# Causal attention core: looks at plain heads moved behind the hyperbolic ones, row maxima turned and laid in two goes

## The chip, the cores and the metric

The program runs on one core of one Trainium2 chip. Its time is device microseconds (us) of that core. The kernel before took 5732.23 us, the median of three runs (5721.1, 5732.23, 5742.0). The engines are named as the profile names them: PE (TensorE matmul), PEld (its weight load), DVE (VectorE), ACT (ScalarE), POOL (GpSimd), SP (SyncE). Each engine works off its own instructions in the order in which they are written, and waits on semaphores for the others.

## The reference

A batch of 32 sequences of 273 tokens by 256 channels passes a patch embedding, a plain causal attention, a quantised feed-forward, then the attention that this change is about, then a second attention (not causal) with a mixture of experts. The attention that matters has 16 heads of three kinds, all causal:

```python
def _hyp_attn(q, k, v, curv):                          # heads 6 to 9
    tq = jnp.sqrt(1.0 / curv + jnp.sum(q * q, axis=-1, keepdims=True))
    tk = jnp.sqrt(1.0 / curv + jnp.sum(k * k, axis=-1, keepdims=True))
    inner = jnp.einsum('bhtd,bhsd->bhts', q, k) - tq * jnp.swapaxes(tk, -1, -2)
    arg = jnp.maximum(-curv * inner, 1.0 + 1e-07)
    dis = jnp.sqrt(1.0 / curv) * jnp.arccosh(arg)
    scores = 1.0 / (eps + dis) + _causal_bias(...)
    return jnp.einsum('bhts,bhsd->bhtd', softmax(scores), v)
outs.append(_sdpa(q[:, :6], k[:, :6], v[:, :6], 1.0 / math.sqrt(HD)))   # heads 0 to 5, plain
outs.append(_hyp_attn(q[:, 6:10], k[:, 6:10], v[:, 6:10], curvature))
outs.append(_sdpa(qn, kn, v[:, 10:], math.sqrt(HD)))                     # heads 10 to 15, q and k of unit length
```

A softmax needs its row maximum subtracted. Heads 10 to 15 need none, since their scores are bounded. For the other ten the kernel finds the maxima of a batch ahead of its main pass.

## The kernel before, in words

`attention_core` runs twice: as "g" (causal, the three kinds, tiles g_...) and as "e" (not causal, all plain, tiles e_...). Both go through 32 batches of three query tiles of 91 tokens. `program` cuts each batch into 16 slots (p = 0 to 15). In slot p every engine's `step` is called three times: "post" for the batch before, "main" for the current one, "pre" for the next. A piece of work has a step number: -16 to -1 is "pre" of that slot plus 16, 0 to 15 is "main", 16 to 31 is "post". An engine's order is thus slot by slot, and in a slot post, main, pre; inside one call it is the order in which `step` is written.

The work of a batch n in "g":

- **Look** at head h (lines 1526 to 1535 for PE, 1656 to 1697 for DVE). PE makes the scores by query into a ring of three PSUM banks, in two units. For a plain head DVE reduces them to the negated row maximum (`g_neg`, L1670, three instructions). For a hyperbolic head DVE reduces (L1668), copies the raw scores by key (L1683), clamps (L1689) and forms the argument of a root (L1694). Then ACT takes the root one slot later (ROOT, L1614 and L1616), DVE adds (SUM, L1700, two slots later) and ACT makes the final score (SCORE, L1619 to L1624, four slots later). Before, the looks are one to a slot in slots 5 to 14 of the batch ahead: 6, 0, 7, 1, 8, 2, 9, 3, 4, 5.
- **Turn and lay** (`shifts`). When the looks are done, DVE negates the hyperbolic maxima (NEGATE, L1703). PE turns all ten rows of maxima (L1546, into PSUM bank 7), ACT casts the high part to bf16 ("hi", L1629, one slot later), DVE subtracts it ("rest", L1708), ACT casts the middle part ("mid", L1632, two slots later), DVE makes the low part ("lo", L1712), and POOL issues three DMAs that lay the parts into extra rows of q (L1474). Before, there is one go: turn in slot 1, hi and rest in slot 2, mid, lo and DMAs in slot 3.
- **Main** pass over `ORDER`. PE makes the head's scores by key into a second ring (waiting for the laid rows unless the head is one of 10 to 15), ACT exponentiates them into `g_probT` (L1603). For a hyperbolic head DVE first adds the shift to the final score (L1654) and ACT exponentiates from there.
- **Product and back.** Four heads form a group g. PE multiplies with v in steps 4g+4 to 4g+6 (L1560), ACT copies the result (`g_oT`, L1610), PE turns it back in step 4g+8 (L1575, again bank 7), and DVE divides by the sums (L1721, L1724; "out"). Groups 2 and 3 fall to slots 0 and 4 of the next batch.

Bank 7 is shared by turn and back, so a turn waits for the last `out`, and a back waits for the last `rest`.

Of the kernel before, what the change touches and what calls it, by code (L numbers as in the profile page):

```python
# [22 lines left out]
H, HD = 16, 16  # L23
# [1244 lines left out]
def attention_core(nc, c, ps, NB, name, kinds, causal, hd, parts_dram, v_dram, ctx_dram, extra_dram=None, curv_dram=None):  # L1268
# [12 lines left out]
    with ctx:  # L1281
# [11 lines left out]
        if causal:  # L1293
            UNITS = 2
            QTILE = {2: (0, 0), 1: (1, 0), 0: (1, 2 * R)}
            KTILE = {0: (0, 0), 1: (1, 0), 2: (1, 2 * R)}
            ORDER = [12, 13, 14, 15, 10, 11, 8, 9, 4, 6, 5, 7, 0, 1, 2, 3]
            HALVES = (1, 0)
        else:
            UNITS = 3  # L1300
            QTILE = {t: (t, 0) for t in range(NT)}
            KTILE = QTILE
            ORDER = list(range(H))
            HALVES = (0, 1)
        HYPS = [h for h in range(H) if kinds[h] == HYP]

        hyp_slot = [[h for h in ORDER if h in HYPS].index(h) for h in HYPS]
        SDPAS = [h for h in range(H) if kinds[h] == SDPA]
        n_hyp = len(HYPS)
        MAXED = n_hyp + len(SDPAS)  # L1310

        def place(step):
            return (("pre", step + H) if step < 0 else ("main", step) if step < H else ("post", step - H))


        first = -11 if n_hyp else -13
        look_order = [h for pair in zip(HYPS, SDPAS) for h in pair] + SDPAS[n_hyp:]
        look_step = {h: first + x for x, h in enumerate(look_order)}
        look = {place(step): h for h, step in look_step.items()}


# [1 line left out]
        if n_hyp:  # L1323

            ROOT, SUM, SCORE = 1, 2, 4
            NEGATE = place(look_step[HYPS[-1]] + SCORE + 1)
            shifts = [(look_step[HYPS[-1]] + SCORE + 2, 0, MAXED)]
        else:
            shifts = [(-7, 0, 6), (-3, 6, 10), (5, 10, H)]
        NSH = len(shifts)  # L1330
# [2 lines left out]
        back_step = {g: 4 * g + 8 for g in range(4)}  # L1333
# [9 lines left out]
        def shifts_at(when, p, later=0):  # L1343

            return [(x, lo, hi) for x, (step, lo, hi) in enumerate(shifts) if place(step + later) == (when, p)]
# [134 lines left out]
        def _(pe):  # L1480
# [32 lines left out]
            def step(when, p, n, u, i):  # L1513
                if when == "main":
                    h = ORDER[p]
                    if kinds[h] != COS:
                        x = [lo <= h < hi for _, lo, hi in shifts].index(True)
# [6 lines left out]
                if (when, p) in look:  # L1524
                    h = look[when, p]
# [10 lines left out]
                for x, lo, hi in shifts_at(when, p):  # L1536
                    done = [y for (h, _, _), y in uses.items() if lo <= h < hi]
                    pe.wait_ge(S["looked"].sem, S["looked"].at(n, max(done) + 1))
                    if n_hyp:
                        pe.wait_ge(S["hneg"].sem, S["hneg"].at(n))  # L1540

                    ways = 4 + max([g for g in back_step if back_step[g] - H < shifts[x][0]], default=-1)
                    pe.wait_ge(S["out"].sem, S["out"].at((n[0], n[1] - 1), ways - 3))
                    pe.wait_ge(S["rest"].sem, S["rest"].at(n, x))
                    for t in range(NT):
                        last = nc.tensor.transpose(ps[0:hi - lo, 7, t * R:(t + 1) * R], neg[:, u, t, lo:hi],  # L1546
                                                   c["ident"][0:R, 0:R])
                    last.then_inc(S["turn"].sem, 1)
                if (when, p) in product:
                    g, kt = product[when, p]  # L1550
# [7 lines left out]
                    for j in range(4 * g, 4 * g + 4):  # L1558
                        a = ORDER[j] % 4
                        last = nc.tensor.matmul(ps[32 * a:32 * a + VW, 6, q0:T], vp[:, u, kt, ORDER[j], :],  # L1560
                                                probT[:, j % 8, b, col:col + T - q0],
# [3 lines left out]
                if (when, p) in back:  # L1565
                    g = back[when, p]
# [10 lines left out]
                    last.then_inc(S["back"].sem, 1)  # L1577

            program(pe, step)

        @block.scalar
        def _(act):
# [7 lines left out]
            def step(when, p, n, u, i):  # L1590
                if when == "main":
                    h = ORDER[p]
                    act.wait_ge(S["pv"].sem, S["pv"].at(n, p // 4 - 1))
# [43 lines left out]
        def _(dve):  # L1637
# [8 lines left out]
            def step(when, p, n, u, i):  # L1646
# [50 lines left out]
                for a, h in enumerate(HYPS):  # L1697
                    if (when, p) == place(look_step[h] + SUM):
                        dve.wait_ge(S["root"].sem, S["root"].at(n, a + 1))
                        nc.vector.tensor_tensor(hw[:, u, a], hw[:, u, a], hu[:, a], ALU.add).then_inc(S["z"].sem, 1)  # L1700
                if n_hyp and (when, p) == NEGATE:
                    dve.wait_ge(S["score"].sem, S["score"].at(n))
# [667 lines left out]
def program(nc, NB, patches, txt, rot, wtok, a_wq, a_wk, a_wv, a_wo, gate_w, up_w, down_w,  # L2370
# [17 lines left out]
    with ctx:  # L2388
# [7 lines left out]
        with ExitStack() as ffn:  # L2396
# [16 lines left out]
            def fix_scale(k):  # L2413
# [14 lines left out]
            run(phase_f1, c, ps, NB, magic[:], o, h1, downT, scale["o"][:], inv["o"][:], wqkv, curv, h2, parts1, extra1,  # L2428
                v1)
        run(attention_core, c, ps, NB, "g", KINDS, True, HD1, parts1, v1, ctx1, extra1, curv)  # L2430
        run(phase_g1, c, ps, NB, ctx1, h2, proj, projb, f_wq, f_wk, f_wv, f_bq, f_bk, f_bv, h3, x3, parts2, v2)
        run(attention_core, c, ps, NB, "e", [SDPA] * H, False, HD, parts2, v2, ctx2)
        run(phase_g3, c, ps, NB, ctx2, x3, h3, f_wo, f_bo, g1, be1, wg, bg, we, bexp, g2, be2, out)

# [37 lines left out]
```

## Time and profile before

| | |
|---|---|
| median of the runs | 5732.23 us (5721.1 to 5742.0) |
| the profiled execution | 5748.39 us, its span 5746.7 us |
| busy over the span | PE 4422.5, PEld 2884.0, DVE 3816.5, ACT 2478.7, POOL 596.5 us |
| the causal core "g" | about 2240 to 3450 us of the span |
| 2600 to 2900 us, inside it | PE 240.84, DVE 209.56, ACT 213.56, POOL 11.98 us busy of 300 |

In the causal core no engine is busy all the time: about 80% for PE and 70% for DVE and ACT. The mean hides that a batch has stretches with different limits, so it is read instruction by instruction in the timeline. There, an entry gives start, duration, engine, line and operation, tile out and in, how many were merged, and in brackets how long the engine had been idle before and who ended that. An engine starts its next instruction about 0.07 us before the printed end of the last.

### The profile page before, as it was taken

Reading aid. Unit: us, or ns where it says so; the run is one execution under the profiler, and the core shown is the slowest. Engines: PE = TensorE matmul, PEld = TensorE weight load, DVE = VectorE, ACT = ScalarE, POOL = GpSimd, SP = SyncE. Lnnn points to the kernel's source line nnn. Section 1 sums busy time; section 2 is a strip of 40 time slices with the busy share of each in tenths; the row PEclk is TensorE's granted clock in tenths of the full one; section 3 lists DMA queues with packets and bytes.
Section 4 is the critical chain, followed back from the end, with each engine's and each line's share of the span. In section 5 each row is a group of like instructions: output and inputs, shape, how many; then the busy total and the mean of one; then the engine's idle time right before and its main releaser. Section 6 shows DMA issues by size and latency. Waiting matters only on the chain. (4 is left out here: it accounts for less than half of the span.)

```text
span 5746.7 us, 99792 instructions
## 1 busy us (share of the span) xinstructions
PE 4422.5 (77%) x26575; PEld 2884.0 (50%) x26575; DVE 3816.5 (66%) x9299; ACT 2478.7 (43%) x5698; POOL 596.5 (10%) x928
## 2 busy tenths in 40 slices
PE   6999788300388885878787776776999998689898
PEld 5777566200255553555555555554555554344444
DVE  4555333588687877777767764555777777477776
ACT  2222333565333333677777762222666666200000
POOL 0111000000000001000000001111111111122221
PEclk9999899655699997777777787887999999899998
DMA  2222233679644443222222225555333333211110
GB/s 81 74 75 68 105 140 139 196 240 396 229 132 124 132 124 91 62 71 71 71 71 71 71 52 144 156 156 139 85 91 92 92 90 88 63 46 47 49 47 25
DMA packets 380380, 617.00 MB, mean 107 GB/s; under 512 B 43575, under 2 KB 310389, under 8 KB 380277
## 3 DMA queue, kind: packets, MB, share of 16 engines
q1 hardware_dynamic: 367956, 614.35, 36.6%
q0 software_dynamic: 12320, 1.40, 0.2%
q8 instruction: 48, 0.79, 0.1%
q14 instruction: 56, 0.45, 0.0%
HBM read 345.02 MB, written 269.21 MB: 107 GB/s over the span
## 5 line engine op out<-in xcount | busy, mean ns | idle before, releaser
L1670 DVE TENSOR_REDUCE e_neg<-ps 91x1 f32<-91x273 f32 x1536 | 571.8, 427 | 139.2 <-PE ps L1491 131.8
L1603 ACT ACTIVATE e_probT<-ps 91x273 f32<-91x273 f32 x1536 | 491.6, 392 | 291.7 <-PE ps L1491 290.9
L1218 PE MATMUL ps<-k_downT,f_o 128*91 128x256 f32 x1152 | 259.7, 385 | 455.9 <-DVE f_o L1126 455.7
L2345 PE MATMUL ps<-m_we,m_xT 128*128 128x512 f32 x1104 | 530.8, 630 | 0.0
L1218 PEld LDWEIGHTS ps<-k_downT,f_o 128*91 128x91 f32 x1152 | 182.8, 161 | 524.5 <-issue 456.9
L1489 PE MATMUL ps<-c_mask_kq,c_identb 91*91 91x91 bf16 x1536 | 322.7, 241 | 105.9 <-ACT g_probT L1603 74.3
L1491 PE MATMUL ps<-e_k,e_q 96*91 96x273 bf16 x1536 | 344.3, 306 | 62.9 <-DMA e_k<-s_parts 28.1
L2279 DVE SCALAR_TENSOR_TENSOR m_acc<-ps,m_weight,m_acc 128x256 f32<-128x256 f32 x552 | 261.7, 481 | 185.7 <-PE ps L2345 175.9
L1491 PE MATMUL ps<-g_q,g_k 102*91 102x273 bf16 (+5 forms) x1536 | 328.5, 294 | 50.6 <-DVEq L1676 49.9
L2345 PEld LDWEIGHTS ps<-m_we,m_xT 128*128 128x128 f32 x1104 | 214.8, 202 | 227.9 <-issue 213.5
L1491 PE MATMUL ps<-e_q,e_k 128*91 128x273 bf16 x1536 | 285.7, 290 | 40.1 <-DMA e_q<-e_shift 38.2
L1489 PEld LDWEIGHTS ps<-c_mask_kq,c_identb 91*91 91x91 bf16 x1536 | 215.4, 150 | 176.7 <-ACT g_probT L1603 128.6
L587 DVE TENSOR_REDUCE b_new<-b_gu 128x1 f32<-128x1638 f32 x64 | 119.0, 1859 | 274.9 <-ACT b_gu L651 274.9
L1491 PEld LDWEIGHTS ps<-e_k,e_q 96*91 96x91 bf16 x1536 | 174.2, 123 | 247.4 <-DVE e_neg L1670 193.1
L1603 ACT ACTIVATE g_probT<-ps 91x273 f32<-91x273 f32 x768 | 262.6, 388 | 44.1 <-PE ps L1491 39.7
L1489 PE MATMUL ps<-c_mask_qk,c_identb 91*91 91x91 bf16 x960 | 215.5, 252 | 76.4 <-DVE g_neg L1670 38.5
L1560 PE MATMUL ps<-g_probT,g_vp 128*32 128x273 f32 (+2 forms) x3072 | 252.3, 409 | 24.3 <-ACT g_probT L1603 24.3
L686 PE MATMUL ps<-b_x,k_gateT 128*128 128x273 f32 x768 | 212.2, 439 | 70.9 <-DVE b_x L663 70.9
L1560 PE MATMUL ps<-e_probT,e_vp 128*32 128x273 f32 x3072 | 258.5, 409 | 9.4 <-ACT e_probT L1603 6.6
L1491 PEld LDWEIGHTS ps<-g_q,g_k 102*91 102x91 bf16 (+1 forms) x1536 | 217.7, 151 | 87.8 <-DVEq L1676 82.3
L651 ACT COPY b_gu<-ps 128x273 f32<-128x273 f32 x384 | 148.8, 388 | 234.6 <-PE ps L686 234.6
L1491 PEld LDWEIGHTS ps<-e_q,e_k 128*91 128x91 bf16 x1536 | 176.2, 124 | 98.3 <-issue 39.5
(306 smaller groups left out, 9733.9 us busy)
## 6 DMA issues: line engine op xcount, KB each, us to landing
s_gate<-b_gu SPq DMA_DIRECT2D x32, 819.0 KB, 4.7
s_up<-b_gu SPq DMA_DIRECT2D x32, 819.0 KB, 6.1
c_g<-s_gate SPq DMA_DIRECT2D x32, 819.0 KB, 7.2
s_gated<-c_g SPq DMA_DIRECT2D x32, 819.0 KB, 8.6
d_g<-s_gated SPq DMA_DIRECT2D x32, 819.0 KB, 10.4
d_u<-s_up SPq DMA_DIRECT2D x32, 819.0 KB, 10.7
s_o<-d_o SPq DMA_DIRECT2D x32, 819.0 KB
f_o<-s_o SPq DMA_DIRECT2D x32, 819.0 KB, 4.8
```

Of the source, the lines that this page charges most:

```text
L587: nc.vector.tensor_reduce(new, x, AX.X, ALU.max, apply_absolute_value=True).then_inc(s_new.sem, 1)
L651: nc.scalar.copy(gu[:, u, m // FT, m % FT, :], ps[:, 4 * u + m % 4, 0:T])\
L686: last = nc.tensor.matmul(ps[:, 4 * u + m % 4, 0:T], w[:, k, (m % FT) * 128:(m % FT + 1) * 128], x[:, u, k, :], start=(k == 0), stop=(k == ...
L1218: last = nc.tensor.matmul(ps[0:R, t // 2, (t % 2) * D:(t % 2 + 1) * D], o[:, u, k, t * R:(t + 1) * R], downT[:, k, :], start=(k == 0), sto ...
L1489: nc.tensor.matmul(ps[0:R, bank, col + col_of_mask:col + col_of_mask + R], c["identb"][0:R, 0:R], c[mask][0:R, 0:R], start=True, stop=Fals ...
L1491: return nc.tensor.matmul(out_, stationary, moving, start=mask is None, stop=True, skip_group_check=mask is not None)
L1560: last = nc.tensor.matmul(ps[32 * a:32 * a + VW, 6, q0:T], vp[:, u, kt, ORDER[j], :], probT[:, j % 8, b, col:col + T - q0], start=(kt == 0 ...
L1603: nc.scalar.activation(probT[0:R, p % 8, b, :], src, ACT.Exp, scale=float(HD) ** 0.5 if kinds[h] == COS else 1.0)\
L1670: last = nc.vector.tensor_reduce(neg[:, u, t, h:h + 1], src, AX.X, ALU.max, negate=True)
L2279: nc.vector.scalar_tensor_tensor(out=acc[:, u, t], in0=ps[0:R, EBANK[m % 4], j * D:(j + 1) * D], scalar=weight[:, u, t, 2 * p + j:2 * p + ...
L2345: last = nc.tensor.matmul(ps[0:R, EBANK[m % 4], :], xT[:, u, k, t * R:(t + 1) * R], we[:, k, 2 * p:2 * p + 2, :].rearrange("p e d -> p (e ...
```

## The change

In the causal core the hyperbolic looks keep their slots (5, 7, 9, 11 of the batch ahead) and nothing stands between them any more. The six plain looks follow in consecutive slots: 4, 5, 0 in slots 13, 14, 15, and 1, 2, 3 in slots 0, 1, 2 of the batch's own main pass. The maxima go in two goes. The first, heads 6 to 9, has the slots of the old one (turn in 1, hi and rest in 2, mid, lo and DMAs in 3). The second, heads 0 to 5, has its turn in slot 4, hi and rest in 5, mid, lo and DMAs in 6. In the main pass slots 8 to 11 hold heads 6, 7, 4, 5 and not 4, 6, 5, 7. The rule for which `out` a turn waits for now counts a group whose back stands in the same slot. For "e", looks, goes and order stay as they were.

```diff
-            ORDER = [12, 13, 14, 15, 10, 11, 8, 9, 4, 6, 5, 7, 0, 1, 2, 3]
+            ORDER = [12, 13, 14, 15, 10, 11, 8, 9, 6, 7, 4, 5, 0, 1, 2, 3]
...
-        first = -11 if n_hyp else -13
-        look_order = [h for pair in zip(HYPS, SDPAS) for h in pair] + SDPAS[n_hyp:]
-        look_step = {h: first + x for x, h in enumerate(look_order)}
+        if n_hyp:
+            look_step = {6: -11, 7: -9, 8: -7, 9: -5, 4: -3, 5: -2, 0: -1, 1: 0, 2: 1, 3: 2}
+        else:
+            look_step = {h: h - 13 for h in range(H)}
+        look_order = sorted(look_step, key=look_step.get)
...
-            NEGATE = place(look_step[HYPS[-1]] + SCORE + 1)
-            shifts = [(look_step[HYPS[-1]] + SCORE + 2, 0, MAXED)]
+            last_hyp = max(look_step[h] for h in HYPS)
+            NEGATE = place(last_hyp + SCORE + 1)
+            shifts = [(last_hyp + SCORE + 2, HYPS[0], MAXED), (max(look_step.values()) + 2, 0, HYPS[0])]
...
-                    if n_hyp:
+                    if n_hyp and lo == HYPS[0]:
                         pe.wait_ge(S["hneg"].sem, S["hneg"].at(n))
 
-                    ways = 4 + max([g for g in back_step if back_step[g] - H < shifts[x][0]], default=-1)
+                    ways = 4 + max([g for g in back_step if back_step[g] - H <= shifts[x][0]], default=-1)
```

**On DVE**, from slot 3 into slot 7 of a batch, before (L1712 is lo, L1721 and L1724 are out, L1668 starts a hyperbolic look, L1654 is the main pass of a hyperbolic head, L1670 a plain look):

```order
 L1712 TENSOR_TENSOR g_shift<-g_rest,g_shift 10x273
 L1721 RECIPROCAL g_rec<-ps 91x12
 L1724 TENSOR_TENSOR g_out<-ps,g_rec 91x3x64
 L1668 TENSOR_REDUCE g_top<-ps 91x1 x3
 L1678 TENSOR_SCALAR g_hw<-g_top,g_negc 91x3
 L1683 TENSOR_SCALAR g_hw<-ps,g_negc 91x273 x2
 L1689 TENSOR_SCALAR g_hw<-g_hw 91x549
 L1694 SCALAR_TENSOR_TENSOR g_hu<-g_hw 91x549
 L1654 TENSOR_TENSOR g_hw<-g_hw,ps 91x273 x2
 L1670 TENSOR_REDUCE g_neg<-ps 91x1 x3
 L1654 TENSOR_TENSOR g_hw<-g_hw,ps 91x273 x2
 L1668 TENSOR_REDUCE g_top<-ps 91x1 x3
```

and now, all lines three or so higher in number (L1711 is rest, L1715 lo):

```order
 L1715 TENSOR_TENSOR g_shift<-g_rest,g_shift 4x273
 L1724 RECIPROCAL g_rec<-ps 91x12
 L1727 TENSOR_TENSOR g_out<-ps,g_rec 91x3x64
 L1711 TENSOR_TENSOR g_rest<-ps,g_shift 6x273
 L1671 TENSOR_REDUCE g_top<-ps 91x1 x3
 L1681 TENSOR_SCALAR g_hw<-g_top,g_negc 91x3
 L1686 TENSOR_SCALAR g_hw<-ps,g_negc 91x273 x2
 L1692 TENSOR_SCALAR g_hw<-g_hw 91x549
 L1697 SCALAR_TENSOR_TENSOR g_hu<-g_hw 91x549
 L1657 TENSOR_TENSOR g_hw<-g_hw,ps 91x273 x2
 L1715 TENSOR_TENSOR g_shift<-g_rest,g_shift 6x273
 L1657 TENSOR_TENSOR g_hw<-g_hw,ps 91x273 x2
```

The second go's rest stands ahead of the look at head 6, its lo between the main passes of heads 8 and 9, and the look at head 0 is gone from there.

**On ACT**, from slot 2 into slot 6, before (L1603 exponentiates, L1629 is hi, L1632 mid, L1610 the copy of a product, L1614 and L1616 the root):

```order
 L1603 ACTIVATE g_probT<-ps 91x273 x2
 L1629 CAST g_shift<-ps 10x273
 L1603 ACTIVATE g_probT<-ps 91x273 x2
 L1632 CAST g_shift<-g_rest 10x273
 L1603 ACTIVATE g_probT<-ps 91x273 x4
 L1603 ACTIVATE g_probT<-g_hw 91x273 x2
 L1610 COPY g_oT<-ps 128x273
 L1614 ACTIVATE g_hu<-g_hu 91x549
```

and now (L1606 exponentiates, L1632 is hi, L1635 mid):

```order
 L1606 ACTIVATE g_probT<-ps 91x273 x2
 L1632 CAST g_shift<-ps 4x273
 L1606 ACTIVATE g_probT<-ps 91x273 x2
 L1635 CAST g_shift<-g_rest 4x273
 L1606 ACTIVATE g_probT<-ps 91x273 x4
 L1632 CAST g_shift<-ps 6x273
 L1606 ACTIVATE g_probT<-g_hw 91x273 x2
 L1613 COPY g_oT<-ps 128x273
 L1635 CAST g_shift<-g_rest 6x273
 L1617 ACTIVATE g_hu<-g_hu 91x549
```

The second hi stands behind the exponentials of slot 5, the second mid behind those of head 8 and the copy of group 0.

**On PE**, in slot 4, before (L1575 is the back of group 3, L1489 and L1491 the scores of head 10, L1560 the product of group 0):

```order
 L1575 MATMUL ps<-c_ident,g_oT 91x128 x3
 L1489 MATMUL ps<-c_mask_kq,c_identb 91x91
 L1491 MATMUL ps<-g_q,g_k 91x273
 L1489 MATMUL ps<-c_mask_kq,c_identb 91x91
 L1491 MATMUL ps<-g_q,g_k 91x182
 L1489 MATMUL ps<-c_mask_kq,c_identb 91x91
 L1491 MATMUL ps<-g_q,g_k 91x91
 L1560 MATMUL ps<-g_probT,g_vp 32x273 x4
```

and now:

```order
 L1578 MATMUL ps<-c_ident,g_oT 91x128 x3
 L1492 MATMUL ps<-c_mask_kq,c_identb 91x91
 L1494 MATMUL ps<-g_q,g_k 91x273
 L1492 MATMUL ps<-c_mask_kq,c_identb 91x91
 L1494 MATMUL ps<-g_q,g_k 91x182
 L1492 MATMUL ps<-c_mask_kq,c_identb 91x91
 L1494 MATMUL ps<-g_q,g_k 91x91
 L1549 MATMUL ps<-c_ident,g_neg 6x91 x3
 L1563 MATMUL ps<-g_probT,g_vp 32x273 x4
```

The second turn stands between the scores of head 10 and the product of group 0, and behind it everything of slots 4 and 5.

## Rows read from the trace of the kernel before

**Rows 1.** The subtraction "rest", L1708: count, ns min/median/max, first and last start, shapes.

```profile
L1708 DVE TENSOR_TENSOR e_rest<-ps,e_shift x96: 418/421/432, 4021.3 to 4911.5; 6x273 f32<-6x273 f32 x64, 4x273 f32<-4x273 f32 x32
L1708 DVE TENSOR_TENSOR g_rest<-ps,g_shift x32: 429/431/432, 2298.9 to 3422.1; 10x273 f32<-10x273 f32 x32
```

**Rows 2.** Timeline of DVE: "rest" in three consecutive batches.

```profile
2663.73 0.43 DVE L1708 TENSOR_TENSOR g_rest<-ps,g_shift 10x273 f32<-10x273 f32 x1 [4.16 <-ACT g_shift L1629]
...
2701.16 0.43 DVE L1708 TENSOR_TENSOR g_rest<-ps,g_shift 10x273 f32<-10x273 f32 x1 [2.61 <-ACT g_shift L1629]
...
2736.63 0.43 DVE L1708 TENSOR_TENSOR g_rest<-ps,g_shift 10x273 f32<-10x273 f32 x1 [2.61 <-ACT g_shift L1629]
```

**Rows 3.** Timeline of DVE, slots 3 to 8 of the batch at 2700 us.

```profile
2702.08 0.43 DVE L1712 TENSOR_TENSOR g_shift<-g_rest,g_shift 10x273 bf16<-10x273 f32 x1 [0.49 <-ACT g_shift L1632]
...
2702.69 0.35 DVE L1724 TENSOR_TENSOR g_out<-ps,g_rec 91x192 f32<-91x192 f32 x1
2704.46 0.44 DVE L1668 TENSOR_REDUCE g_top<-ps 91x1 f32<-91x273 f32 x1 [1.42 <-PE ps L1491]
...
2708.18 0.78 DVE L1654 TENSOR_TENSOR g_hw<-g_hw,ps 91x273 f32<-91x273 f32 x2
...
2709.64 0.78 DVE L1654 TENSOR_TENSOR g_hw<-g_hw,ps 91x273 f32<-91x273 f32 x2
...
2713.94 0.72 DVE L1700 TENSOR_TENSOR g_hw<-g_hw,g_hu 91x549 f32<-91x549 f32 x1
...
2715.11 0.84 DVE L1670 TENSOR_REDUCE g_neg<-ps 91x1 f32<-91x273 f32 x3
```

**Rows 4.** Timeline of ACT, slots 2 to 13 of the same batch.

```profile
2699.83 0.39 ACT L1610 COPY g_oT<-ps 128x273 f32<-128x273 f32 x1 [0.31 <-PE ps L1560]
2700.11 0.68 ACT L1603 ACTIVATE g_probT<-ps 91x273 f32<-91x273 f32 x2
2700.68 0.36 ACT L1629 CAST g_shift<-ps 10x273 bf16<-10x273 f32 x1
...
2701.63 0.42 ACT L1632 CAST g_shift<-g_rest 10x273 bf16<-10x273 f32 x1
...
2703.51 0.68 ACT L1603 ACTIVATE g_probT<-ps 91x273 f32<-91x273 f32 x2 [0.42 <-PE ps L1491]
2708.64 0.78 ACT L1603 ACTIVATE g_probT<-g_hw 91x273 f32<-91x273 f32 x2 [4.45 <-DVE g_hw L1654]
...
2717.02 0.74 ACT L1619 ACTIVATE g_hw<-g_hw,g_one 91x549 f32<-91x549 f32 x1
...
2719.23 0.66 ACT L1603 ACTIVATE g_probT<-ps 91x273 f32<-91x273 f32 x2
...
2726.06 0.66 ACT L1614 ACTIVATE g_hu<-g_hu 91x549 f32<-91x549 f32 x1 [0.39 <-DVE g_hu L1694]
...
2727.32 0.66 ACT L1603 ACTIVATE g_probT<-ps 91x273 f32<-91x273 f32 x2
```

**Rows 5.** Timeline of PE, slots 1 to 6 of the same batch.

```profile
2699.07 0.40 PE L1546 MATMUL ps<-c_ident,g_neg 91*10 91x91 f32 x3
...
2701.65 0.56 PE L1575 MATMUL ps<-c_ident,g_oT 128*91 128x128 f32 x3 [0.67 <-DVE g_rest L1708]
...
2702.51 0.67 PE L1560 MATMUL ps<-g_probT,g_vp 128*32 128x273 f32 x8
2703.11 0.24 PE L1489 MATMUL ps<-c_mask_kq,c_identb 91*91 91x91 bf16 x1
...
2704.06 0.24 PE L1489 MATMUL ps<-c_mask_qk,c_identb 91*91 91x91 bf16 x1
...
2704.47 0.28 PE L1491 MATMUL ps<-g_q,g_k 102*91 102x273 bf16 x1
...
2706.52 0.24 PE L1489 MATMUL ps<-c_mask_kq,c_identb 91*91 91x91 bf16 x1 [1.20 <-DMA g_q<-g_shift]
```

**Rows 6.** Stretch of slots 1 to 4 one batch earlier: us, engines' busy, PEclk, DMA.

```profile
2659.70:2667.20 7.50, 6.92 (x57) 4.49 (x50) 1.45 (x4) 4.23 (x12) 1.49 (x3) 0.50 0.47 134
```

## The prediction

> **What bounds the kernel now.** I read the page first: it shows that only the causal core "g" holds what the diff touches. Then the source view of one instruction that comes once per batch, to have the period, then the timelines of DVE, ACT and PE over one batch, to see what sets it. "rest" runs 32 times from 2298.9 to 3422.1 us [rows 1], so the mean period is 1123.2 / 31 = 36.23 us. One batch took 35.47 us (2701.16 to 2736.63), the one ahead of it 37.43 us [rows 2]. I walk through the shorter kind.
>
> A batch has two halves. From slot 5 DVE is the limit: the look at head 6 starts at 2704.46, and from there DVE has no wait but those inside a look until sum and back at 2713.94 and the plain look at 2715.11, and it goes on so to about 2726 [rows 3]. ACT stands waiting for it, 4.45 us at 2708.64, still 0.39 us at 2726.06 [rows 4]. From slot 12 or 13 ACT is the limit, and DVE idles: 2.61 us at each "rest" [rows 2]. In slots 2 to 5 the path is short-linked through three engines: product on PE, its copy on ACT at 2699.83 (waited 0.31 us for PE), exponentials, hi at 2700.68 [rows 4], rest on DVE at 2701.16 [rows 2], back on PE at 2701.65 (waited 0.67 us for rest), product 2702.51, scores 2703.11, product, look 2704.06 [rows 5], DVE at 2704.46 after 1.42 us idle [rows 3]. So both halves are on the path, and the joint between them too. What is taken off DVE's half counts only until something else is late, and what is put into slots 0 to 5 has no cover but small gaps.
>
> **The change part by part**, for one batch, with PE at the faster clock. Start to start is the printed length less about 0.07 us. Times under 100 are counted from 2700 us.
>
> 1. Looks 1, 2 and 3 come onto PE in slots 0, 1, 2. A look's first unit takes 2704.06 to 2704.47 = 0.41 us, and I count its three pairs of matmuls at 0.41 (the scores of same size took up to 0.50, 2703.11 on) [rows 5]. Look 1 mostly falls into PE's gaps, look 2 stands ahead of the turn at 2699.07 and the product that ACT waits for already, look 3 is covered by PE's 0.67 us wait for rest. I take +0.45 at ACT's copy (bounds: 0, if all fits in the gaps; 1.2, three looks in full). DVE has 2.6 us idle there, so its part costs nothing. The plain looks 4, 5, 0 in slots 13 to 15 lie under ACT's work and cost nothing; should that cover go, a look is 0.76.
>
> 2. The second turn, slot 4. It waits for `out` of group 3 in the same slot. `out` ends at 2702.69 + 0.35 = 2703.04 [rows 3], seen by PE at about 2703.10; PE is there at 2702.51 [rows 5]: wait 0.60, then the transposes, 0.40 - 0.07 = 0.33. Queued behind: the product of group 0, the scores and product of slot 5, and look 6, for which DVE waits. +0.93 (bounds 0.33 without wait, 1.5 at the slower clock).
>
> 3. The second rest, slot 5, stands ahead of look 6 on DVE, and waits for a hi that stands behind the exponentials of slot 5 on ACT. With parts 1 and 2 the scores start at 2703.11 + 1.38 = 4.49, the exponentials 0.40 later at 4.89 (from 2703.11 to 2703.51), hi 0.57 later at 5.46 (2700.11 to 2700.68), its end 5.82, rest at 5.94 (the lag from 2700.68 + 0.36 to 2701.16 is 0.12). Look 6 would be there at 2704.46 + 1.38 = 5.84. Rest takes 0.43 - 0.07 = 0.36; that it has 6 rows and not 10 saves nothing, the 4 and 6 row ones of "e" take 421 ns against 431 [rows 1]. Look 6 starts at 6.30: +1.84 in all so far.
>
> 4. Look 0 leaves slot 6: -0.76 (2708.18 to 2709.64 is 1.46, of it 0.70 the main pass) [rows 3].
>
> 5. The second lo stands between the main passes of heads 8 and 9 and waits for mid, which stands behind ACT's exponentials of head 8 and the copy. Main pass 8 starts at 2708.18 + 1.84 = 10.02, is over at 10.72. ACT starts 0.46 after its start (2708.18 to 2708.64), takes 0.70 + 0.28, mid 0.42: 11.88 [rows 4]. Lo at 11.9: DVE stands for 1.2 us and works 0.36. Before, nothing stood there. +1.55 (bounds 0.36 if mid came in time, 2.8 if the root, 1.26 from 2726.06 to 2727.32, also stood ahead; the order rules that out). The main pass of head 9 and all the hyperbolic looks are behind it.
>
> 6. Looks 1 and 2 leave slots 8 and 10: -1.52. At the end of slot 11 DVE is 1.84 - 0.76 + 1.55 - 1.52 = 1.1 later than before.
>
> 7. ACT. Heads 6 and 7 now come in slots 8 and 9, so the exponentials of head 6 wait for DVE's sum (0.65) and main pass before the root of head 7 can start, where plain head 4 used to pass early. Look 7 starts at 12.98, ends 3.60 later (slot 7 from 2709.64 + 0.70 to 2713.94) at 16.58, sum at 17.22, exponentials of head 6 at 17.68. From there ACT has no gap: exponentials of 6 and 7 2 x 0.70, roots of 7, 8, 9 3 x 1.26, scores of 6 and 7 2 x 2.21 (2717.02 to 2719.23), exponentials of 4, 5, 0 3 x 0.57, copy 0.28 [rows 4] = 11.6, end at 29.3. Before, that point was 2727.32. **+1.9 us per batch**, of which 1.1 is DVE's and 0.8 that ACT now ends last.
>
> The first laid rows land 0.45 later than 2706.52 [rows 5], while look 6 lasts beyond 2710: nothing. The second go's are needed only in slot 10: nothing. POOL's three more DMAs: nothing waits for them. First and last batch: DVE's opening run loses four plain looks, 3 us, the last slots gain a turn and lo; I set them to zero together.
>
> 31 x 1.9 = 59 us. Against the profiled execution, 5748.4 + 59 = 5807; that one lies 16 us above the median of the runs, so for the median 5732 + 59 = 5791.
>
> **The rivals.**
> - *The clock.* In slots 1 to 4 ahead of the long period the granted clock was 0.50, the lower of its two levels (1.2 of 2.4 GHz) [rows 6], though PE was busy 6.92 of 7.50 us. The period then was 37.43, not 35.47 [rows 2]; in the mean the clock costs 36.23 - 35.47 = 0.76 per batch. With more PE work on the path of slots 0 to 5, and PE thinner in DVE's half, it may cost more. If every batch were of the long kind, +1.2 x 31 = 37 us more: 5828. Against it: in the mean before only 0.76 of the 1.96 was paid. The Trainium skill, "TensorE: Matmul & The Clock Gate", section "HAM oscillation", lets the clock fall after idle gaps of PE and rise when it is busy. By that rule the thinner PE of slots 6 to 11 would favour this rival, and the sum would be the 5828; the row agrees only in part, since the clock was low in a busy stretch.
> - *No change.* Mid comes in time for lo, and ACT keeps its slack: DVE's end is then 1.1 - 1.2 = -0.1 per batch, 5729. For it: ACT idles 4.45 us ahead of slot 6. Against: mid stands behind exponentials that wait for DVE itself.
> - *Faster*, the other side: the moved looks pay and the second go is hidden wholly, in slots 4 to 6. The place is DVE from slot 5 to 11: -2.28 for looks 0, 1, 2, +0.72 for rest and lo. It decides if the waits of parts 2, 3 and 5 (0.60, 0.1, 1.2) and the PE time of parts 1 and 2 vanish. -1.56 x 31 = -48: 5684. For it: DVE is without a gap there. Against: the three instructions stand where the other engine is just not done.
>
> **How the numbers follow.** Forecast 0.60, clock 0.14, no change 0.12, faster 0.14. The forecast's own range: without ACT's 0.8, +34, 5766; with the upper bounds of parts 1 and 2, +1.3 more per batch, but not both at once, 5815. The range to hold 8 in 10 reaches from near the case of no change to the clock case: 5718 to 5830. A change under 0.3% (17 us) can't be told from none. Faster by more 0.15, within 0.12, slower 0.73.
>
> **What would show it.** In the timeline after: a second "rest" on DVE directly ahead of look 6, with an idle time released by ACT's cast; a lo between two L1657 with about 1.2 us idle, released by the cast; PE waiting some 0.6 us ahead of the 6-row turn for `out`; ACT without a wait from the exponentials of head 6 to those of head 1; DVE's old idle time at the first rest shrinking by the looks in it. The period, from the first 4-row rest to the last over 31, would be about 38.1 us. I am wrong if lo shows no idle time, or if the period falls below 36.2; and wrong in a size if the long kind of batch becomes the rule or vanishes.

## The result and the profile after

The changed kernel takes 5837.5 us, the median of four runs (5830.94 to 5846.66), the kernel before 5735.08 (5721.1 to 5742.0, four runs): ratio 1.0183, 95% interval 1.0159 to 1.0207. It is slower by 1.8%, on the side that was forecast, but the cost is 102 us where 59 were predicted, and the time lies 7.5 us above the stated range. The profiled execution took 5846.66 us with a span of 5844.8.

The period first. The first go's rest starts at 2303.0 us in the first batch and at 3526.6 in the last: (3526.6 - 2303.0) / 31 = 39.47 us, against 36.23 [rows 1]: 3.24 us per batch and 100 us in all, so all of it is in the causal core. As before there are short and long batches. The timeline of DVE, three rests in a row:

```profile
2696.49 0.42 DVE L1711 TENSOR_TENSOR g_rest<-ps,g_shift 4x273 f32<-4x273 f32 x1
...
2734.84 0.42 DVE L1711 TENSOR_TENSOR g_rest<-ps,g_shift 4x273 f32<-4x273 f32 x1
...
2774.99 0.42 DVE L1711 TENSOR_TENSOR g_rest<-ps,g_shift 4x273 f32<-4x273 f32 x1
```

Here the period is the distance from the first go's rest to the next one, and the last of these starts is at 3526.61 in the timeline; the source view's last start, 3532.3, is that of a second go. The short kind is 38.35 us (before 35.47 [rows 2]), the long kind 40.15 (before 37.43). So +2.88 in the batch that the prediction walked through, where it had +1.95 (its 1.9). Now the joint between the halves, on DVE (here L1711 is rest, L1715 lo, L1727 out, L1671 a look's first instruction, L1657 the main pass of a hyperbolic head):

```profile
2697.39 0.43 DVE L1715 TENSOR_TENSOR g_shift<-g_rest,g_shift 4x273 bf16<-4x273 f32 x1 [0.48 <-ACT g_shift L1635]
...
2698.00 0.35 DVE L1727 TENSOR_TENSOR g_out<-ps,g_rec 91x192 f32<-91x192 f32 x1
2702.20 0.43 DVE L1711 TENSOR_TENSOR g_rest<-ps,g_shift 6x273 f32<-6x273 f32 x1 [3.85 <-ACT g_shift L1632]
2702.56 0.42 DVE L1671 TENSOR_REDUCE g_top<-ps 91x1 f32<-91x273 f32 x1
...
2706.15 0.78 DVE L1657 TENSOR_TENSOR g_hw<-g_hw,ps 91x273 f32<-91x273 f32 x2
2708.01 0.43 DVE L1715 TENSOR_TENSOR g_shift<-g_rest,g_shift 6x273 bf16<-6x273 f32 x1 [1.08 <-ACT g_shift L1635]
2708.37 0.77 DVE L1657 TENSOR_TENSOR g_hw<-g_hw,ps 91x273 f32<-91x273 f32 x2
```

Before, look 6 began 3.30 us after rest (2704.46 - 2701.16 [rows 2, 3]); now 6.07 (2702.56 - 2696.49): +2.77. The second rest stands directly ahead of it, as forecast, but after 3.85 us of idle time. Why hi came so late is on ACT (L1606 exponentiates, L1632 is hi, L1635 mid):

```profile
2699.73 0.68 ACT L1606 ACTIVATE g_probT<-ps 91x273 f32<-91x273 f32 x2 [1.33 <-PE ps L1494]
2701.70 0.38 ACT L1632 CAST g_shift<-ps 6x273 bf16<-6x273 f32 x1 [1.29 <-DMA g_q<-g_shift]
2706.61 0.78 ACT L1606 ACTIVATE g_probT<-g_hw 91x273 f32<-91x273 f32 x2 [4.53 <-DVE g_hw L1657]
...
2707.56 0.41 ACT L1635 CAST g_shift<-g_rest 6x273 bf16<-6x273 f32 x1
...
2713.75 0.78 ACT L1606 ACTIVATE g_probT<-g_hw 91x273 f32<-91x273 f32 x2 [3.88 <-DVE g_hw L1657]
...
2725.21 0.66 ACT L1606 ACTIVATE g_probT<-ps 91x273 f32<-91x273 f32 x2
```

At 2701.70 hi had waited 1.29 us, and not for ACT's own work: for the DMA `g_q<-g_shift`, the laying of the first go. The exponentials ahead of it began at 2699.73 and their printed end is 2700.41. And PE (L1578 back, L1549 turn, L1563 product, L1492 and L1494 scores and looks):

```profile
2696.96 0.56 PE L1578 MATMUL ps<-c_ident,g_oT 128*91 128x128 f32 x3 [0.70 <-DVE g_rest L1711]
...
2698.41 0.40 PE L1549 MATMUL ps<-c_ident,g_neg 91*6 91x91 f32 x3 [0.51 <-DVE g_out L1727]
2698.74 0.67 PE L1563 MATMUL ps<-g_probT,g_vp 128*32 128x273 f32 x8
...
2703.09 0.46 PE L1494 MATMUL ps<-g_q,g_k 102*91 102x182 bf16 x2 [2.12 <-DVEq L1679]
```

The turn at 2698.41 waited 0.51 us for `out`, where 0.60 was predicted, and the product comes 0.33 behind it, as predicted. But then PE stands 2.12 us in the middle of look 6, since DVE can't take its first unit.

Three stretches make up a period: from the first go's rest to the start of look 6 (the joint), from there to the end of the root of head 9 (DVE's full half, and the first part of ACT's), and from there to the next rest. Taken from the timelines over all 31 periods, their means are, in us:

| | joint | middle | last | period |
|---|---|---|---|---|
| before | 3.89 | 22.81 | 9.54 | 36.23 |
| after | 6.34 | 23.02 | 10.11 | 39.47 |
| e1 (below) | 4.72 | 23.23 | 9.82 | 37.77 |

So 2.45 of the 3.24 us that a batch takes more are in the joint.

### The profile page after: what moved, and what is told of

Its sections match the earlier page's. It is cut to its first block and busy times, and to the rows that moved or that the text cites. A ratio compares the mean times of both kernels' runs of the same rounds, so it can differ in the third digit from the quotient of the medians.

```text
span 5844.8 us, 100532 instructions
## 1 busy us (share of the span) xinstructions
PE 4442.7 (76%) x26671; PEld 2895.7 (50%) x26671; DVE 3851.1 (66%) x9363; ACT 2479.7 (42%) x5762; POOL 646.4 (11%) x1024
## 3 DMA queue, kind: packets, MB, share of 16 engines
q0 software_dynamic: 15392, 1.42, 0.2%
## 5 line engine op out<-in xcount | busy, mean ns | idle before, releaser
L1606 ACT ACTIVATE e_probT<-ps 91x273 f32<-91x273 f32 x1536 | 491.5, 392 | 290.4 <-PE ps L1494 290.1
L1492 PE MATMUL ps<-c_mask_kq,c_identb 91*91 91x91 bf16 x1536 | 345.3, 252 | 159.6 <-ACT g_probT L1606 155.5
L1494 PE MATMUL ps<-g_q,g_k 102*91 102x273 bf16 (+5 forms) x1536 | 356.6, 306 | 120.6 <-DVEq L1679 116.4
L1494 PE MATMUL ps<-e_k,e_q 96*91 96x273 bf16 x1536 | 343.4, 305 | 62.4 <-DMA e_k<-s_parts 27.5
L1492 PEld LDWEIGHTS ps<-c_mask_kq,c_identb 91*91 91x91 bf16 x1536 | 223.6, 156 | 250.8 <-ACT g_probT L1606 205.8
L1494 PE MATMUL ps<-e_q,e_k 128*91 128x273 bf16 x1536 | 285.6, 290 | 37.2 <-DMA e_q<-e_shift 35.5
L1494 PEld LDWEIGHTS ps<-g_q,g_k 102*91 102x91 bf16 (+1 forms) x1536 | 228.9, 158 | 157.6 <-DVEq L1679 155.6
L1494 PEld LDWEIGHTS ps<-e_k,e_q 96*91 96x91 bf16 x1536 | 173.7, 123 | 248.2 <-DVE e_neg L1673 193.9
L1606 ACT ACTIVATE g_probT<-ps 91x273 f32<-91x273 f32 x768 | 257.7, 386 | 70.7 <-PE ps L1494 69.9
L1563 PE MATMUL ps<-e_probT,e_vp 128*32 128x273 f32 x3072 | 260.1, 411 | 11.5 <-ACT e_probT L1606 8.7
L1563 PE MATMUL ps<-g_probT,g_vp 128*32 128x273 f32 (+2 forms) x3072 | 258.8, 419 | 8.6 <-ACT g_probT L1606 8.6
L1673 DVE TENSOR_REDUCE g_neg<-ps 91x1 f32<-91x273 f32 (+2 forms) x576 | 164.4, 337 | 99.7 <-PE ps L1494 98.1
L1477 POOL DMA_DIRECT2D e_q<-e_shift x288 | 143.9, 506 | 769.9 <-DVE e_shift L1715 764.1
```

The costliest lines, as they stand in the source:

```text
L1477: pool.dma_start(q[rows + part:rows + part + 1, u, lo:hi, :], shift[0:hi - lo, u, part, :]).then_inc(laid[u], 16)
L1492: nc.tensor.matmul(ps[0:R, bank, col + col_of_mask:col + col_of_mask + R], c["identb"][0:R, 0:R], c[mask][0:R, 0:R], start=True, stop=Fals ...
L1494: return nc.tensor.matmul(out_, stationary, moving, start=mask is None, stop=True, skip_group_check=mask is not None)
L1606: nc.scalar.activation(probT[0:R, p % 8, b, :], src, ACT.Exp, scale=float(HD) ** 0.5 if kinds[h] == COS else 1.0)\
L1673: last = nc.vector.tensor_reduce(neg[:, u, t, h:h + 1], src, AX.X, ALU.max, negate=True)
```

## The wait that was missed

The cast hi writes `g_shift`, the buffer from which POOL's DMAs lay the parts into q. Its guard is in a line that the diff doesn't touch:

```python
act.wait_ge(laid[u], 16 * PARTS * (NSH * i + x))
nc.scalar.copy(shift[0:hi - lo, u, 0], ps[0:hi - lo, 7, 0:T]).then_inc(S["hi"].sem, 1)
```

With one go, x is 0 and the count is that of the batch two before, long landed. With two, the second go (x = 1) waits until the first go of the same batch has landed in q, and that go's DMAs are issued only in slot 3, two slots ahead of the second hi. The source view of L1632 adds up ACT's idle time ahead of it, after and then in e1 (below), where each go has its own buffer and the instruction is L1638:

```profile
L1632 ACT CAST g_shift<-ps x64: 358/369/380, 2302.2 to 3531.9; 4x273 bf16<-4x273 f32 x32, 6x273 bf16<-6x273 f32 x32
...
  DMA g_q<-g_shift: 47.1, 32
```

```profile
L1638 ACT CAST g_shift<-ps x64: 358/360/363, 2294.8 to 3470.3; 4x273 bf16<-4x273 f32 x32, 6x273 bf16<-6x273 f32 x32
...
  PE ps L1553: 34.0, 1
  DMA e_q<-e_shift: 15.6, 4
```

47.1 us over 32 batches after, none of it in e1.

## The experiments

All were run against the kernel before on the same chip; ratios are to it, with the 95% interval. The prediction's chip had it at 5735 us, the others at 5743 to 5757, so ratios say more than medians.

**e1, a buffer for each go.** `own(u, x)` picks one of two buffers, and hi waits only for the last use of its own:

```diff
-        shift = sb("shift", [H, 2, PARTS, T], BF16)
+        shift = sb("shift", [H, 2 * (2 if n_hyp else 1), PARTS, T], BF16)
...
-                    act.wait_ge(laid[u], 16 * PARTS * (NSH * i + x))
+                    used = NSH * i + x - (NSH - 1 if n_hyp else 0)
+                    if not isinstance(used, int) or used > 0:
+                        act.wait_ge(laid[u], 16 * PARTS * used)
```

> The changed kernel, with a buffer of its own for the cast parts of each go, so that ACT's second hi no longer waits for the DMAs of the first go of the same batch (in the changed trace it waits up to 1.4 us per batch, released by the laying DMA; the prediction had overlooked this wait). Theory A, this wait is what the prediction missed: the wait at the second hi is gone, the period falls by about 1.3 us, 31 x 1.3 = 40 us, to about 5797 us, near the 5791 of the prediction. Rival (the clock): the excess over the prediction came from more batches at the lower clock, and the time stays at 5825 to 5837. Rival (hidden): the wait is under another one on the same path, gain under 10 us.

Measured: 5786.6 us, ratio 1.0087 (1.0053 to 1.0120). The wait is worth 51 us of the 102 by the medians of two chips, 55 us by the ratios (0.0183 - 0.0087 of 5735). The 5791 us that were predicted without it are a ratio of 1.0103, inside the interval. The clock's rival of 5825 us or more is refuted as the cause of the whole excess. The timeline of ACT in e1, hi behind the exponentials at once and so without an idle time:

```profile
2715.46 0.68 ACT L1610 ACTIVATE g_probT<-ps 91x273 f32<-91x273 f32 x2 [1.33 <-PE ps L1498]
2716.03 0.36 ACT L1638 CAST g_shift<-ps 6x273 bf16<-6x273 f32 x1
```

It starts 2716.03 - 2715.46 = 0.57 us behind the start of the exponentials, the lag that the prediction took. On DVE (L1717 is rest, L1677 a look's first instruction) and ACT, the joint and the end of the middle stretch of the same batch:

```profile
2712.21 0.42 DVE L1717 TENSOR_TENSOR g_rest<-ps,g_shift 4x273 f32<-4x273 f32 x1
2716.63 0.43 DVE L1717 TENSOR_TENSOR g_rest<-ps,g_shift 6x273 f32<-6x273 f32 x1 [2.54 <-ACT g_shift L1638]
2716.99 0.42 DVE L1677 TENSOR_REDUCE g_top<-ps 91x1 f32<-91x273 f32 x1
...
2730.62 0.44 DVE L1677 TENSOR_REDUCE g_top<-ps 91x1 f32<-91x273 f32 x1 [0.87 <-PE ps L1498]
...
2740.18 0.66 ACT L1610 ACTIVATE g_probT<-ps 91x273 f32<-91x273 f32 x2
```

The joint is 2716.99 - 2712.21 = 4.78 us, where the changed kernel has 6.07 in a short and 6.30 in a long batch. Over all batches it fell by 6.34 - 4.72 = 1.62, and the period by 39.47 - 37.77 = 1.70: nearly all of the gain is the wait itself, and it is there in every batch. The periods of the short kind hide this. That of e1 is 37.49 us, only 38.37 - 37.49 = 0.88 less than in the changed kernel, because e1 has another middle stretch, 2740.18 - 2716.99 = 23.19 against 22.65. That is the length that it has in the changed kernel's long batches, with the same wait of 0.87 us for PE at look 8. The granted clock in the second part of that stretch is lower too, in the changed kernel's short batch and then in e1 (columns of [rows 6]):

```profile
2713.30:2725.20 11.90, 9.66 (x82) 6.26 (x83) 10.03 (x27) 11.23 (x23) 0.00 (x0) 0.63 0.00 0
2727.71:2740.18 12.47, 10.88 (x89) 7.20 (x89) 10.14 (x28) 11.34 (x24) 0.00 (x0) 0.55 0.00 0
```

The walk gave 35.47 + 1.95 = 37.42 for the short batch, 0.07 from the 37.49. That close a match is in part luck: the middle came out 0.2 longer than walked and the last stretch 0.1 shorter. In the mean e1 has only 37.77 - 36.23 = 1.54 more than the kernel before.

**e2, looks back in their old slots**, two goes and the new order:

```diff
-            look_step = {6: -11, 7: -9, 8: -7, 9: -5, 4: -3, 5: -2, 0: -1, 1: 0, 2: 1, 3: 2}
+            look_step = {6: -11, 0: -10, 7: -9, 1: -8, 8: -7, 2: -6, 9: -5, 3: -4, 4: -3, 5: -2}
...
-            shifts = [(last_hyp + SCORE + 2, HYPS[0], MAXED), (max(look_step.values()) + 2, 0, HYPS[0])]
+            shifts = [(last_hyp + SCORE + 2, HYPS[0], MAXED), (4, 0, HYPS[0])]
```

> The changed kernel with the looks back in their old slots (6, 0, 7, 1, 8, 2, 9, 3, 4, 5 in slots 5 to 14 of the batch ahead); two goes and the new order of the main pass stay. Theory A, the second go is what costs and the moved looks pay a part of it: per batch +0.9 (turn and its wait for out), +0.5 (rest ahead of look 6), +1.3 (hi behind the first go's DMA), +1.4 (lo and its wait) against before, nothing given back: +4.1 x 31 = 127 us, about 5862, slower than the changed kernel. Rival: the moved looks cost (PE work in slots 0 to 2), then this is faster than the changed kernel, 5800 or less.

Measured: 5881.0 us, 1.0240 (1.0206 to 1.0273). The second go, with the new order, costs even more by itself (+2.4%), and the moved looks give about 0.6% of it back. That the looks were the cost is refuted.

**e3, the order of the main pass alone.**

```diff
-            ORDER = [12, 13, 14, 15, 10, 11, 8, 9, 4, 6, 5, 7, 0, 1, 2, 3]
+            ORDER = [12, 13, 14, 15, 10, 11, 8, 9, 6, 7, 4, 5, 0, 1, 2, 3]
```

> The kernel before with only the order of the main pass changed, heads 6, 7, 4, 5 in slots 8 to 11 and not 4, 6, 5, 7. Theory A: the exponentials of head 6 wait for DVE in slot 8, the root of head 7 starts later, but ACT has 0.2 to 0.9 us gaps behind it and ends no later: within 5 us of before, about 5735. Rival (the prediction's part 7 read strictly): ACT ends 0.8 us later per batch, +25 us, 5760.

Measured: 5755.0 us, 1.0017 (0.9997 to 1.0036): no clear cost. The rival's 25 us would be 1.0044, outside the interval.

**e6, e7, e8: the second go later.** All have e1's buffers. The second go's steps (turn, hi, rest, mid, lo) stand in slots 4, 5, 5, 6, 6 in e1; in e6 in 4, 5, 5, 7, 8; in e7 in 4, 5, 6, 7, 8; in e8 in 5, 6, 7, 7, 8. For e6 the offsets from the turn become a pair, one for each go:

```diff
-                for x, lo, hi in shifts_at(when, p, 2):
+                for x, lo, hi in shifts_at(when, p, (2, 4)):
                     dve.wait_ge(S["mid"].sem, S["mid"].at(n, x + 1))
...
-                for x, lo, hi in shifts_at(when, p, 1):
+                for x, lo, hi in shifts_at(when, p, (1, 2)):      # e7 and e8, rest
                     dve.wait_ge(S["hi"].sem, S["hi"].at(n, x + 1))
...
-            shifts = [(last_hyp + SCORE + 2, HYPS[0], MAXED), (4, 0, HYPS[0])]
+            shifts = [(last_hyp + SCORE + 2, HYPS[0], MAXED), (5, 0, HYPS[0])]      # e8
```

> As e1 (changed kernel, a buffer of its own for each go), with the second go's mid in slot 7 and its lo and DMAs in slot 8, behind work that is done by then. Theory A: the wait at lo between the main passes of heads 8 and 9, 1.1 us per batch, is on the path; without it 31 x 1.1 = 34 us less than e1, 5753. Rival (ACT is the limit from slot 8 on and the wait is hidden): within 8 us of e1, 5787. Rival: laying is now late for head 4 in slot 10, PE waits on the DMA there, and it is no faster than e1.

> As e6, with the second rest moved from slot 5 (ahead of look 6 on DVE) to slot 6 (behind the main pass of head 8). Theory A: look 6 starts 0.46 us earlier, but rest's 0.36 us stay in DVE's half, so 0.1 us per batch, 3 us: within 8 of e6. Rival (rest's place ahead of look 6 holds PE's ring and so more than its own length): 14 us or more less than e6.

> As e7, and the second turn in slot 5 and not 4, hi in slot 6, rest and mid in slot 7, lo in slot 8. Theory A: PE no longer stands 0.5 us at the turn for `out` of group 3, which is long done: 31 x 0.5 = 16 us less than e7, about the time of the kernel before, 5735. Rival (the wait is covered by ACT's or DVE's own): equal to e7 within 8 us.

Measured: e6 5763.1 us, 1.0046 (1.0027 to 1.0065); e7 5753.2, 1.0027 (1.0015 to 1.0040); e8 5746.4, 1.0001 (0.9987 to 1.0014). From e1 to e6 the ratio falls by 0.0041 (24 us, 34 were expected; the intervals just overlap), from e7 to e8 by 0.0026 (15 us, 16 expected). From e6 to e7 it falls by 0.0019, within the noise of both, and lies between its theory and its rival: what moving rest is worth stays open. The profiled periods fall in the same order, 37.77 in e1, then 36.78, 36.48 and 36.23 us. In e8 the two goes take no more time than the one of the kernel before. That doesn't make the second go free, since e8 also has what the moved looks gain: against e9 below (0.9929, one go, the same order, one look still in slot 8) it is 0.7% or 41 us slower, where the changed kernel is 2.5% or 146 us slower. So most of the second go's cost was not its work but where its instructions stood. In e6 DVE goes from the main pass of head 6 into lo without idle time:

```profile
2719.55 0.78 DVE L1664 TENSOR_TENSOR g_hw<-g_hw,ps 91x273 f32<-91x273 f32 x2
2720.25 0.42 DVE L1722 TENSOR_TENSOR g_shift<-g_rest,g_shift 6x273 bf16<-6x273 f32 x1
```

**e4, e5, e9, e12: one go, looks moved.** Old order, but for e9:

```diff
-            look_step = {6: -11, 7: -9, 8: -7, 9: -5, 4: -3, 5: -2, 0: -1, 1: 0, 2: 1, 3: 2}
+            look_step = {6: -11, 7: -9, 0: -8, 8: -7, 9: -5, 1: -4, 2: -3, 3: -2, 4: -1, 5: 0}
...
-            shifts = [(last_hyp + SCORE + 2, HYPS[0], MAXED), (max(look_step.values()) + 2, 0, HYPS[0])]
+            shifts = [(last_hyp + SCORE + 2, 0, MAXED)]
```

e9 has these looks and the new order. e5 and e12 differ from e4 in

```diff
-            look_step = {6: -11, 7: -9, 0: -8, 8: -7, 9: -5, 1: -4, 2: -3, 3: -2, 4: -1, 5: 0}
+            look_step = {6: -11, 7: -9, 8: -7, 9: -5, 0: -4, 1: -3, 2: -2, 3: -1, 4: 0, 5: 1}
...
-            shifts = [(last_hyp + SCORE + 2, 0, MAXED)]
+            shifts = [(2, 0, MAXED)]      # e12 alone
```

> One go as in the kernel before (turn in slot 1), old order of the main pass, and only the looks moved: hyperbolic 6, 7, 8, 9 in slots 5, 7, 9, 11 as ever, look 0 alone between them in slot 8, looks 1, 2, 3, 4 in slots 12 to 15 and look 5 in slot 0. Against before two plain looks leave DVE's full half. Theory A: a look taken out of that half is worth its 0.76 us, and PE and DVE have room for it in slots 12 to 0: -1.4 x 31 = -43 us, about 5692. Rival (moved looks cost what they save, PE's work in slots 15 and 0 being on the path): 5735 within 10. Rival: ACT bounds both halves, same result, but with ACT without idle time from slot 9 on.

> As e4, one go and the old order of the main pass, but all six plain looks outside DVE's full half: 0, 1, 2, 3 in slots 12 to 15, 4 in slot 0, 5 in slot 1, so that the turn in slot 1 comes right behind look 5. Theory A: DVE's half falls by another 0.76 us, but PE now stands at the turn until DVE has reduced look 5, about 0.8 us, and the product that ACT waits for stands behind it: no better than e4, 5690 to 5715. Rival (looks are free outside that half): another 0.76 x 31 = 24 us less than e4, 5675.

> As e4 (one go, five plain looks outside DVE's full half), with the new order of the main pass, 6, 7, 4, 5 in slots 8 to 11. Against the changed kernel what is left out is the second go, and one look stands in slot 8 again. Theory A, the three parts of the change add up, and the order costs what it cost alone (e3, +8 us): about 5707; the second go is then worth some 120 us in the changed kernel. Rival: with DVE's half shorter the order makes ACT the limit (0.8 us per batch), 5725 to 5735.

> As e5, six plain looks outside DVE's full half, the last in slot 1, with the one turn a slot later, in slot 2, so that PE doesn't stand at it. Theory A: the 1.0 us that PE waited at the turn in e5 is gone, but hi, rest and lay come a slot later, and the back of group 3 behind rest with them (0.6 to 0.8 us): between e4 and e5, 5715. Rival: the wait at the turn was all that e5 lost, 5680. Rival: laying comes too late for head 8 in slot 6, 5740 or more.

Measured: e4 5698.6 us, 0.9929 (0.9905 to 0.9953), faster than the kernel before; e5 5740.8, 0.9999 (0.9986 to 1.0013); e9 5715.4, 0.9929 (0.9903 to 0.9954); e12 5713.7, 0.9924 (0.9898 to 0.9950). In e4 a short batch took 34.46 us on DVE, 1.0 less than before, for two looks of 0.76; in the mean it was 36.23 - 34.84 = 1.39 less. e5 missed its 5690 to 5715: the third look's gain is lost at the turn, and that of the other two with it. PE, and ACT behind it:

```profile
2730.81 0.40 PE L1549 MATMUL ps<-c_ident,g_neg 91*10 91x91 f32 x3 [0.99 <-DVE g_neg L1673]
```

```profile
2731.56 0.39 ACT L1613 COPY g_oT<-ps 128x273 f32<-128x273 f32 x1 [1.62 <-PE ps L1563]
```

PE waited 0.99 us for look 5, and ACT 1.62 for the product behind the turn (before 0.31 [rows 4]). e12 gets this back with the turn a slot later. By its ratio it is at e4's level and not between e4 and e5: the 5715 expected on 5735 would be 0.9965, outside its interval, the rival's 5680 would be 0.9904, inside. So the turn explains all that e5 lost against e4, but the third look still brought nothing that can be told from noise. e9 against e4: the new order costs nothing there either.

**e10, e11: hyperbolic looks earlier.** Against e4, first e10, then e11 (its turn in slot 1 as in e4):

```diff
-            look_step = {6: -11, 7: -9, 0: -8, 8: -7, 9: -5, 1: -4, 2: -3, 3: -2, 4: -1, 5: 0}
+            look_step = {6: -12, 7: -9, 0: -8, 8: -7, 9: -5, 1: -4, 2: -3, 3: -2, 4: -1, 5: 0}
...
+            look_step = {6: -12, 7: -10, 8: -8, 9: -6, 0: -5, 1: -4, 2: -3, 3: -2, 4: -1, 5: 0}
```

> As e4, with look 6 one slot earlier, in slot 4 of the batch ahead, and its root, sum and score likewise. In e4 DVE is idle for 1.42 us ahead of look 6 and waits for PE, which has scores and product of slot 5 (0.95 us) in front of it. Theory A: DVE's full half starts 0.95 us earlier and ends as much earlier: 31 x 0.95 = 29 us less than e4, 5670. Rival: what follows (main pass of head 8, held by the laid rows until slot 6) does not come earlier, and DVE idles later instead: within 8 of e4, 5699.

> As e10 for all four hyperbolic looks: 6, 7, 8, 9 in slots 4, 6, 8, 10, and the six plain looks in slots 11 to 15 and 0, one go with its turn in slot 1. Theory A: DVE's full half loses the last plain look (0.76) as well and starts 0.95 earlier, and the turn waits for no look: 1.7 x 31 = 53 us less than e4, 5646, if ACT keeps up. Rival: ACT becomes the limit (its work from the exponentials of head 6 to the root of head 9 has no gap left), 5665 to 5700.

Measured: e10 5686.3 us, 0.9885 (0.9861 to 0.9908), the fastest of all, 1.15% under the kernel before. By ratio it gains 0.44% over e4, 25 us, where 29 were expected; the two intervals just overlap. DVE's idle time ahead of look 6 is down from 1.42 us [rows 3]:

```profile
2713.68 0.44 DVE L1671 TENSOR_REDUCE g_top<-ps 91x1 f32<-91x273 f32 x1 [0.47 <-PE ps L1494]
```

e11 5945.2 us, 1.0339 (1.0314 to 1.0365), the worst of all, and no theory had it. Its DVE:

```profile
2733.25 0.78 DVE L1657 TENSOR_TENSOR g_hw<-g_hw,ps 91x273 f32<-91x273 f32 x2
2736.85 0.23 DVE L1724 RECIPROCAL g_rec<-ps 91x12 f32<-91x12 f32 x1 [2.83 <-issue]
...
2737.39 0.43 DVE L1671 TENSOR_REDUCE g_top<-ps 91x1 f32<-91x273 f32 x1
```

The division of group 0 stands in slot 8. In the other kernels DVE comes to it with look 7 behind it and finds the back ready. In e11 look 7 is a slot earlier, DVE comes to it straight from the main pass of head 9, and needs there what PE, ACT and PE make from that very pass (exponentials, product, copy, back): 2.83 us in which DVE stands in its full half. (The view names no releaser; that it was the back is read from PE's times below, 2735.81 + 0.95 = 2736.76.) PE went the same way, waiting 3.23 us for ACT ahead of the scores that precede the product:

```profile
2734.19 0.31 PE L1492 MATMUL ps<-c_mask_kq,c_identb 91*91 91x91 bf16 x1 [3.23 <-ACT g_probT L1606]
...
2734.74 1.14 PE L1563 MATMUL ps<-g_probT,g_vp 128*32 128x273 f32 x8
2735.81 0.95 PE L1578 MATMUL ps<-c_ident,g_oT 128*91 128x128 f32 x3
```

This wait is not all. The period of e11 is (3617.8 - 2299.0) / 31 = 42.54 us, 7.7 more than in e4. The source view of the division, L1724, with its idle time over the whole kernel, shows most of that at the divisions, in e11 and then in e4:

```profile
  PE ps L1578: 147.4, 81
  issue: 103.6, 62
```

```profile
  PE ps L1578: 56.5, 46
  issue: 15.7, 31
```

That is 251.0 against 72.2 us, 179 of the 247 us between the medians. The mean granted clock from 2500 to 3300 us was 0.67 in e11 and 0.78 in e4, so slower matmuls may have a part in it, as cause or as consequence; no run took the two apart.

## Why the prediction was right or wrong

- *What bounds the kernel*: right. The two halves and the joint are there: a wait taken out of the joint (e1) and looks taken out of DVE's half (e4) both moved the time.
- *Part 1, looks on PE*, +0.45: from the root of head 9 done (27.32 before [rows 4], 2725.21 after) to rest it is 9.31 before (2736.63 - 2727.32) and 9.63 after (2734.84 - 2725.21): +0.32. Right, a little large.
- *Part 2, the second turn*, +0.93: 0.51 + 0.33 = 0.84. Right.
- *Part 3, rest ahead of look 6*: here the prediction failed. It took hi to start 0.57 us behind the start of the exponentials of slot 5, and rest to add 0.46 us. Hi started 2701.70 - 2699.73 = 1.97 behind them, because it also waits for the landing of the first go: 1.29 us of idle time in the batch shown and 47.1 / 32 = 1.47 in the mean. Parts 2 and 3 together gave the joint 0.93 + 0.46 = 1.39; it grew by 2.77, and in e1, without the wait, by 4.78 - 3.30 = 1.48. The failing sentence is the one behind part 7: "The first laid rows land 0.45 later than 2706.52 [rows 5], while look 6 lasts beyond 2710: nothing." It asked only who reads the laid rows in q, and not who waits to write their source again.
- *Part 5, lo*: idle 1.08 us and released by mid, predicted 1.2. Right.
- *Parts 4, 6, 7*: from the start of look 6 to the end of the root of head 9 it was 22.86 us before and is 22.65 after (2725.21 - 2702.56), where the walk had 22.97, so 0.32 too much. ACT runs without a wait from 2713.75 on, as forecast.
- *The sum*: 2.77 - 0.21 + 0.32 = 2.88 for the short batch, where the walk had 1.39 + 0.11 + 0.45 = 1.95. The joint missed by 1.38, and the other two gave 0.45 of it back. The rest is the mix of batches: the mean lay 0.76 over the short batch before and 39.47 - 38.35 = 1.12 now, +0.36 or 11 us.
- *The rival of the clock* was right in the 11 us of that mix and named the wrong place. In the kernel before, most batches of the long kind lose their time in the joint (5.32 us against 3.30 in the timelines). In the changed kernel the granted clock of the joint is 1.00 in both kinds, and it is 6.07 against 6.30 us long. Of the 1.80 us between the two kinds, 0.23 lie there, 23.18 - 22.65 = 0.53 in the middle and 10.67 - 9.63 = 1.04 in the last stretch, slots 12 to 2, where the looks 4, 5, 0 now stand, which the prediction had costed at nothing under ACT's work. The windows view, with the columns of [rows 6]: the last stretch of the short batch, then the second part of the middle and the last stretch of the long one:

```profile
2725.20:2734.80 9.60, 8.34 (x113) 6.53 (x110) 6.25 (x22) 8.96 (x23) 0.00 (x0) 0.93 0.40 96
2752.00:2764.00 12.00, 10.55 (x81) 6.82 (x81) 9.85 (x26) 11.02 (x23) 0.00 (x0) 0.50 0.00 0
2764.00:2775.00 11.00, 9.36 (x118) 6.97 (x110) 6.28 (x23) 9.47 (x24) 0.00 (x0) 0.84 0.33 84
```

In the last stretch the granted clock is 0.93 of full speed in the short batch and 0.84 in the long one, so a longer share at the lower of the two levels (1.2 and 2.4 GHz). What that does shows in slot 0, on the product of group 3 and the back of group 2, first in the short batch and then in the long one:

```profile
2729.55 0.67 PE L1563 MATMUL ps<-g_probT,g_vp 128*32 128x273 f32 x8 [0.35 <-ACT g_probT L1606]
2730.15 0.56 PE L1578 MATMUL ps<-c_ident,g_oT 128*91 128x128 f32 x3
```

```profile
2768.77 1.14 PE L1563 MATMUL ps<-g_probT,g_vp 128*32 128x273 f32 x8
2769.84 0.95 PE L1578 MATMUL ps<-c_ident,g_oT 128*91 128x128 f32 x3
```

What decides the level in a given batch was not settled: no run changed the clock alone. The Trainium skill ("TensorE: Matmul & The Clock Gate", section "HAM oscillation") has the clock fall behind idle gaps of PE. These rows don't bear that out as the whole cause: at 0.50 PE was busy 10.55 of 12 us.
- *No change* and *faster* were refuted as forecasts for this kernel, but e8 and e4 come near to what they described: with the waits gone the second go costs about what the moved looks give, and with one go the moved looks pay.

## What to carry to other kernels

When a step that ran once per batch is made to run twice, look at every wait that counts its uses, also in lines that the diff leaves alone: a buffer that was free for a whole batch is now free only when the first use has drained, a DMA's landing included. Moving work out of the full half of a bounding engine paid most of what its instructions last (e4: 1.39 of 1.52 us in the mean), but only into slots where nobody queues behind it; before an in-order engine's instruction is moved, ask what it will find done when it arrives (e11). A period walked from one batch was right to 0.1 us in its sum (e1) once all its waits were in it, though its stretches were off by up to 0.2, so here a gap of half the effect was a missing wait. Compare means over all batches, stretch by stretch: the short batches of two kernels differed by 0.88 us where the wait between them was worth 1.6.

## What was not expected of the hardware

A stretch of a batch keeps its length over most of the core, and yet it is not the same in two kernels that differ elsewhere: the middle stretch of e1 is 23.19 us in nearly every batch, that of the changed kernel 22.65 in most short ones and 23.18 in most long ones, at a granted clock of 0.55 in e1 against 0.63 in the short ones in its second part, though e1 changes nothing in that stretch. The eight matmuls of one product, the same in every batch, took 0.67 us in one batch and 1.14 in the next. The kernels' periods repeat in patterns of short and long batches; the pattern, and not only the work, changed with each edit.
